# A two-layer attention kernel on one core: the first layer's output goes to channel rows by DMA instead of by TensorE transposes

## What is computed

```python
# layer 0
xm  = rmsnorm(x) * (1 + scale) + shift          # scale, shift from cond @ w_cond
q, k, v = split(xm @ w_qkv); q, k = rope(q), rope(k)
o   = softmax(q k^T / 4) v                      # per batch and head, 512 x 512 scores
x1  = o @ w_out + x
# layer 1
q, k, v = layer_norm(x1) @ (q_w, k_w, v_w) + biases
y   = softmax(q k^T + mask) v
out = x1 + silu(layer_norm(y) * (1 + scale1) + shift1) @ out_w + out_b
```

## Time and profile before

| | |
|---|---|
| median of 3 runs | 514.0 us (513.84 to 514.3) |
| the profiled execution | 513.65 us |
| its span, first to last instruction | 511.9 us |
| PE, PE's weight loads, DVE, ACT, POOL busy | 501.6, 193.7, 408.6, 345.7, 219.9 us |
| mean granted TensorE clock | 0.997 |

### The profile page before, as it was taken

The page is one execution under the profiler, slowest core; times in us unless marked ns, Lnnn a source line. Parts: engine busy times, 40 slices in busy tenths (PEclk is TensorE's granted clock), DMA queues, the critical chain, the costliest instruction groups (busy, mean ns, idle before and its releaser), DMA issues.

```text
span 511.9 us, 9839 instructions
## 1 busy us (share of the span) xinstructions
PE 501.6 (98%) x3339; PEld 193.7 (38%) x3339; DVE 408.6 (80%) x1051; ACT 345.7 (68%) x679; POOL 219.9 (43%) x254
## 2 busy tenths in 40 slices
PE   9999899999999999999999999999999999999997
PEld 5553423333443244333443334332433333333234
DVE  4876897998897688966898678967899999999324
ACT  1552467776767675776768676777778778787863
POOL 3039749999143420832227430544573035005401
PEclk9999999999999999999999999999999999999999
DMA  6983232242214133110331123210431112211011
GB/s 243 351 273 101 75 103 75 66 143 82 77 53 125 41 125 121 46 43 8 119 125 44 42 90 114 68 33 32 125 124 44 43 43 85 81 46 44 2 41 42
DMA packets 43034, 45.26 MB, mean 88 GB/s; under 512 B 4436, under 2 KB 41572, under 8 KB 42600
## 3 DMA queue, kind: packets, MB, share of 16 engines
q1 hardware_dynamic: 42696, 42.79, 26.8%
q10 hardware_dynamic: 288, 1.84, 0.9%
HBM read 25.46 MB, written 18.87 MB: 87 GB/s over the span
## 4 chain that ended last, share of the span: by engine, by line
PE 74%; DVE 13%; issue 3%; ACT 2%; POOL 2%; DVEq 0%; ACTq 0%; POOLq 0%
PE bank L547 19%; PE bank L530 11%; PE bank L521 10%; PE bank L593 9%; PE bank L510 9%; DVE masked L870 8%; PE bank L621 5%; PE bank L604 5%; PE bank L562 2%; PE bank L582 2%; DVE row_max L873 1%; ACT probs L721 1%; PE bank L555 1%; PE bank L629 1%; POOL XN L844 1%
## 5 line engine op out<-in xcount | busy, mean ns | idle before, releaser
L721 ACT ACTIVATE probs<-bank 128x512 f32<-128x512 f32 x512 | 272.4, 601 | 82.0 <-PE bank L521 81.3
L873 DVE TENSOR_REDUCE row_max<-bank 128x1 f32<-128x512 f32 x256 | 163.0, 684 | 29.5 <-PE bank L530 27.8
L530 PE MATMUL bank<-k_s,q_s 64*128 64x512 f16 x512 | 183.0, 382 | 1.8 <-DVE row_max L873 1.2
L870 DVE CUSTOM_DVE_ANT_0 masked<-bank,mask_bias 128x512 bf16<-128x512 f32 x256 | 163.0, 687 | 13.0 <-PE bank L530 12.0
L510 PE MATMUL bank<-q_s,k_s 64*128 64x512 f16 x512 | 151.9, 381 | 0.9 <-ACT v_aug L789 0.5
L521 PE MATMUL bank<-shift,kx 64*128 64x512 f16 x512 | 148.8, 377 | 0.0
L547 PE MATMUL bank<-probs,v_aug 128*17 128x512 f32 x1024 | 135.4, 598 | 0.7 <-ACT probs L721 0.7
L530 PEld LDWEIGHTS bank<-k_s,q_s 64*128 64x128 f16 x512 | 46.3, 93 | 151.7 <-DVE row_max L870 67.1
L593 PE MATMUL bank<-xT,wqkv 128*128 128x512 f32 x128 | 61.8, 613 | 0.4 <-ACT xT L752 0.3
L521 PEld LDWEIGHTS bank<-shift,kx 64*128 64x128 f16 x512 | 46.9, 95 | 31.9
L510 PEld LDWEIGHTS bank<-q_s,k_s 64*128 64x128 f16 x512 | 31.7, 94 | 13.4 <-ACT probs L721 8.0
(11 more groups left out here) (112 smaller groups left out, 505.1 us busy)
## 6 DMA issues: line engine op xcount, KB each, us to landing
q_parts<-parts SPq DMA_DIRECT2D x64, 128.0 KB
k_parts<-parts SPq DMA_DIRECT2D x64, 128.0 KB
q_s<-q_parts SPq DMA_DIRECT2D x32, 256.0 KB, 2.8
k_s<-k_parts SPq DMA_DIRECT2D x32, 256.0 KB, 3.0
X<-in_x SPq DMA_DIRECT2D x4, 512.0 KB, 7.3
y<-X SPq DMA_DIRECT2D x7, 256.0 KB, 2.2
wc<-in_w_cond ACTq DMA_DIRECT2D x1, 1024.0 KB, 4.9
tables<-in_tables SPq DMA_DIRECT2D x4, 256.0 KB, 6.8
```

The source lines that it names most:

```text
L530: nc.tensor.matmul(bank, m.q_s[slot][rows, i, queries], m.k_s[slot][rows, i, :], start=True, stop=True).then_inc(q.d_made, 1)
L721: act.activation(m.probs[k][:, h, :], bank, ACT.Exp, scale=1.0 if s >= B * NG else float(DH) ** -0.5)\
L870: dve.tensor_tensor_reduce(m.masked[D["max", n, k, h] % ND][:, :], bank, m.mask_bias[:, b, :], 1.0, LOWEST, ALU.add, ALU.max, to)\
L873: dve.tensor_reduce(to, bank, AX.X, ALU.max).then_inc(q.d_done, 1)
```

## The change

1. **No turns for layer 0's output.** Of groups 0 to 15 the output is no longer transposed. SP sends `oT` as it stands, 4 transfers of 16 rows by 2 KB, to rows of the tile `raw` (the old `O` buffers in another shape), where each channel has its own row, and one small transfer that lays out the 64 rows' sums as 128x16 (`raw_output`). DVE takes their reciprocal at tile k = 3 (`invert`). SP stores the reciprocals to DRAM (`inverses_out`) and loads them spread over the channels' rows (`inverses_in`). POOL multiplies, two products of 128x512 a batch (`divide`), straight into `xT`. The eight transposes of `turn f0` and their ACT copies are gone too.
2. **Where the products stand.** `y` of batch b moves from (5+4b, 2) and (5+4b, 3) to (6+4b, 0) and (6+4b, 1), and waits for `divided`, not for ACT. `turn p1`, `qk` and `v` of layer 1 move about three tiles later.
3. **POOL sends the parts.** The stores of `parts` of the batches 1 to 7, 4 for each of 28 calls, are issued by POOL behind each rope and split. Those of batch 0 stay with SP.
4. **Two `divide` in the rope list** (behind the second and third rope of batch 3), two in each `project(b)` below the last, and `add_bias(LAST, 1)` goes behind the first `negate`.

```diff
+    PIECES[_s] = (*one(y(0, _b)), _other, ())
+    PIECES[_s + 1] = ((), (), turn("p1", _b), qk(1, _b, 0))
+    PIECES[_s + 2] = (*one(qk(1, _b, 1, 2)), qk(1, _b, 3), ())
+    PIECES[_s + 3] = (v(1, _b)[:1], (), (), ())
+PIECES[20] = (*one(qk(1, LAST, 1, 2)), qk(1, LAST, 3), v(1, LAST)[:1])
+PIECES[21] = (v(1, LAST)[1:], (), (), ())
...
-        if op == "output" and k == 2 and s:
+        if op == "output" and k == 2 and s > LAYER:
             yield op, s - 1
+        if op == "output" and k == 3 and 0 < s <= LAYER:
+            yield "sums", s - 1
...
     def tokens_out(piece):
-                pe.wait_ge(q.a_done, turned(USES[use]))
+                pe.wait_ge(q.divided, normalised(b, CT - 1))
...
+    def invert(s):
+        dve.wait_ge(q.sums_in, 16 * (s + 1))
+        if s:
+            dve.wait_ge(q.inv_out, 16 * s)
+        dve.reciprocal(m.inv_sum[:, :, :, :].rearrange("p t h w -> p (t h w)"), m.sums[:, :]).then_inc(q.inv_made, 1)
...
+    def send_parts(pu, i):
+        send_part(pool, m, q, pu, i, 0)
+        pool.wait_ge(q.part_pool, 4 * (pu - 1) + i + 1)
+        send_part(pool, m, q, pu, i, 1)
...
+    def divide(b, c):
+        use = USES.index(("f0", b))
+        pool.wait_ge(q.output_out, group_out(NG * b + 2 * c + 1))
+        pool.wait_ge(q.inv_in[c], 32 * (b + 1))
+        await_read(pool, q, use - 2)
+        pool.tensor_tensor(m.xT[use % 2][:, c, :], m.raw[b % 2][:, c, :], m.inverse[c][:, :], ALU.mult)\
+            .then_inc(q.divided, 1)
...
             rope(b, i)
+            if b == B - 1 and i in (1, 2):
+                divide(0, i - 1)
...
+    def raw_output(s):
+        b, g = divmod(s, NG)
+        sp.wait_ge(q.acc_copied, s + 1)
...
+        sp.dma_start(m.sums[:, :], m.oT[DH::W32, :].rearrange("h (c n) -> h c n", n=KT * G)).then_inc(q.sums_in, 16)
...
+            sp.dma_start(m.raw[b % 2][first + DH * h:first + DH * (h + 1), g // 2, :],
+                         m.oT[W32 * h:W32 * h + DH, :]).then_inc(q.output_out, 16)
...
     for s in range(-1, GROUPS + 2):
+        if 0 < s <= LAYER:
+            raw_output(s - 1)
         if exists(s + 1):
             shift(s + 1)
         if s >= 0 and exists(s + 3):
             operands(s + 3)
-        for pu, i in PARTS_AT.get(s, ()):
-            parts(pu, i)
+        if 0 < s <= LAYER:
+            inverses_out(s - 1)
+        if 0 < s <= LAYER:
+            inverses_in(s - 1)
```

More of the change, by code:

```diff
@@ L29 @@
 GROUPS = LAYERS * B * NG
+LAYER = B * NG
 UNIT = 64.0
@@ L388, in build @@
         q.acc_copied = sem("acc_copied")
+        q.output_out = sem("output_out")
+        q.sums_in = sem("sums_in")
+        q.inv_out = sem("inv_out")
+        q.inv_in = [sem(f"inv_in{i}") for i in range(CT)]
+        q.divided = sem("divided")
         q.shift_high = sem("shift_high")
@@ L447, in build @@
         q.x_in = [sem(f"x_in{b}") for b in range(B)]
+        q.first_out = [sem(f"first_out{i}") for i in range(4)]
         q.parts_out = [sem(f"parts_out{i}") for i in range(4)]
@@ L480, in d_bank, with await_parts @@
     return m.d_banks[place % ND]
-def chunk_out(pu):
-    return 64 * (pu + 1)
+def await_parts(engine, q, pu, i):
+    if pu:
+        engine.wait_ge(q.parts_out[i], 64 * pu)
+    else:
+        engine.wait_ge(q.first_out[i], 64)
 def half(h):
@@ L567, in turn_tokens @@
         bank = d_free(D[piece]) if kind == "f1" else a_free(A[piece])
-        if kind == "f0":
-            pe.wait_ge(q.d_done, D["output", NG * b + NG - 1] + 1)
-            src = m.O[b % 2]
-        else:
-            n = NORMAL.index((kind, b))
-            src = m.XN[n % 2]
-            if h == 0 and n == 0:
-                pe.wait_ge(q.ident_made, 4)
-                pe.wait_ge(q.xn0_made, TPB)
-            elif h == 0 and n == len(NORMAL) - 1:
-                pe.wait_ge(q.xn0_made, 2 * TPB)
-            elif h == 0:
-                pe.wait_ge(q.xn_made, TPB * n)
+        n = NORMAL.index((kind, b))
+        src = m.XN[n % 2]
+        if h == 0 and n == 0:
+            pe.wait_ge(q.ident_made, 4)
+            pe.wait_ge(q.xn0_made, TPB)
+        elif h == 0 and n == len(NORMAL) - 1:
+            pe.wait_ge(q.xn0_made, 2 * TPB)
+        elif h == 0:
+            pe.wait_ge(q.xn_made, TPB * n)
         for t in range(TPB):
@@ L1074, in vector @@
                 negate(n)
+        if op == "sums":
+            invert(*at)
         if op == "output":
@@ L1244, in project @@
         normal("p1", b)
+        if b < LAST:
+            divide(b + 1, 0)
         at = m.X[:, TPB * b:TPB * b + TPB, :]
@@ L1253, in project @@
         add_bias(b, 0)
+        if b < LAST:
+            divide(b + 1, 1)
     pool.wait_ge(q.late_in, 64)
@@ L1258, in gpsimd @@
         project(b)
-    add_bias(LAST, 1)
     def negate(n):
@@ L1276, in gpsimd @@
         negate(NG * (B + b) + 6)
+        if b == 0:
+            add_bias(LAST, 1)
         rstd("f1", b)
@@ L1292, in gpsimd @@
             .then_inc(q.last_rstd, 1)
-def send_parts(engine, m, q, pu, i):
-    for part in range(2):
-        send_part(engine, m, q, pu, i, part)
 def send_part(engine, m, q, pu, i, part):
@@ L1306, in send_part @@
         to = m.k_dram[pu, heads, copy, part, dims, :] if i >= 2 else m.q_dram[pu, heads, part, copy, dims, :]
-        engine.dma_start(to, m.parts[:, part, i, :]).then_inc(q.parts_out[i], 16)
+        engine.dma_start(to, m.parts[:, part, i, :]).then_inc((q.parts_out if pu else q.first_out)[i], 16)
 def sync(sp, m, q):
@@ L1359, in shift, with inverses_out, inverses_in @@
                 .then_inc(q.shift_in[n % SHIFTS], 16)
+    def raw_output(s):
+        b, g = divmod(s, NG)
+        sp.wait_ge(q.acc_copied, s + 1)
+        if b >= 2:
+            sp.wait_ge(q.divided, normalised(b - 2, g // 2))
+        if s:
+            sp.wait_ge(q.inv_made, s)
+        sp.dma_start(m.sums[:, :], m.oT[DH::W32, :].rearrange("h (c n) -> h c n", n=KT * G)).then_inc(q.sums_in, 16)
+        first = chunk_rows(g).start
+        for h in range(G):
+            sp.dma_start(m.raw[b % 2][first + DH * h:first + DH * (h + 1), g // 2, :],
+                         m.oT[W32 * h:W32 * h + DH, :]).then_inc(q.output_out, 16)
+    def inverses_out(s):
+        sp.wait_ge(q.inv_made, s + 1)
+        sp.dma_start(m.inv_dram[s].rearrange("h (c n) -> (h c) n", n=KT * G),
+                     m.inv_sum[:, :, :, :].rearrange("p t h w -> p (t h w)")).then_inc(q.inv_out, 16)
+    def inverses_in(s):
+        b, g = divmod(s, NG)
+        sp.wait_ge(q.inv_out, 16 * (s + 1))
+        sp.wait_ge(q.part_dve, 4)
+        if g % 2 == 0 and b:
+            sp.wait_ge(q.divided, normalised(b - 1, g // 2))
+        sp.dma_start(m.inverse[g // 2][chunk_rows(g), :], m.inv_dram[s].unsqueeze(1).broadcast_to([G, DH, S]))\
+            .then_inc(q.inv_in[g // 2], 16)
     def output(b, j):
```

56 lines of the change are left out of this document (29 added, 27 removed).

## The result

The changed kernel takes 516.15 us (median of 8 runs, 514.94 to 520.68) against 514.02 for the kernel before in the same session: a ratio of 1.0057, 95% interval 1.003 to 1.0085. It is slower, as forecast, but by 2.1 us and not by 9, and not for the reason that I gave. The profiled execution has a span of 514.3 us; before it was 511.9. One single run behind this page, of the second padding in experiment 2, took 623.17 us at a granted clock of 0.748, and its ratio leaves that run out.

The account below looks back on a forecast made before the run. PE was taken to bound the kernel, with 74% of the chain of waits. 513.65 - 12.1 (turns) + 18.3 (wait for `divide`) + 1.6 (group 22) + 1.5 (clock) = 523.0 us, range 502 to 534.

Parts of the forecast that it names:

- Twelve microseconds go from PE: PE, layer 0: 16 output turns at 0.5 us and four turns back, together 12.1 us gained.
- I take no more than 0.5 us off for that: DVE loses one 0.43 us product a group; where it bounds a plain step it gives back nearly the same.
- DVE above 13% of the chain, gain below 10: Sign in the profile after: if seen, with the gain being PE's, DVE's room was put too high.
- The new way if POOL were free: Output path through SP, DVE and reciprocals: ready near 133, PE at the product at 137.6; cost nothing.
- SP is the late one: Rival: SP blocked ahead of `shift`, PE waiting 1 to 2 us in 8 to 16 steps; 510 to 534 us; chance 0.06.
- POOL's price: POOL's time c to issue one store, 112 issues: taken as 0.95 us, from bounds 0.6 to 1.13.
- 18.3 us of the sum: First product with w_out: PE waits 18.3 us for POOL's second `divide`, which ends at 155.9.
- the rival: POOL's issue is cheap, c 0.6 or less: wait 0 to 3 us; 501.5 to 511 us; chance 0.30; decides at c = 0.78.
- POOL's half of that working: POOL's second `divide` at the first product with w_out ends at 114.1 + 44c, 155.9 with c = 0.95.
- PE's half, 137.6: PE reaches the first product with w_out at 137.6, against 135.45 in the kernel before.
- Group 22's negation, 1.6 us: Layer 1, batch 3: POOL's `negate` ends at 29.7, PE needs it at 28.1; one wait of 1.6 us.
- The clock, 1.5 us: Behind the 18 us wait PE's clock may start low, near 1.2 GHz, for two to four microseconds; cost 1.5 us.

Follow-up runs that it names:

- second padding: Kernel before, with SP issuing five extra transfers of 16 rows by 2 KB ahead of `shift` in steps 1 to 16: 518.1 us, ratio 1.0071.
- experiment 2: Kernel before, five extra SP transfers ahead of `shift` in steps 1 to 16: small ones 514.27 us, ratio 1.0002; 16 rows by 2 KB 518.1 us, 1.0071.
- exp. 3: Kernel before, one transpose in place of four in each output turn of groups 0 to 15 and each turn back: 510.62 us, ratio 0.9933.
- exp. 1: Changed kernel, SP's order with `raw_output` last: 518.86 us, ratio 1.0094; with `operands` first, then `shift`, `raw_output` (the version meant): 509.09 us, 0.9900.
- exp. 5: Kernel before with POOL sending parts, plus one wait on POOL: 515.4 us, ratio 1.0024. Changed kernel with two POOL fills behind each of twelve ropes: 529.51 us, 1.0296.
- exp. 6: Changed kernel, `operands` first, three POOL waits: 510.86 us, ratio 0.9936; with a fourth wait and second `divide` ahead of the third rope: 505.06 us, 0.9823.
- exp. 4: Kernel before with POOL sending the parts of batches 1 to 7: 517.24 us, ratio 1.006. Changed kernel with SP sending them again: 527.32 us, 1.0254.

## Why the prediction went wrong

**Twelve microseconds go from PE.** The instructions went. Their worth did not follow: "I take no more than 0.5 us off for that". PE's time alone reached the end at 3.6 of 9.1 us, or of 7.9 by the timelines (exp. 3); even the best version gets 9.0 of 12.1. The earlier trace rows had shown DVE busy 10.85 of 11.50 us, and I wrote down the limit, 0.65 us a step, and compared it with one turn of 0.5. It should have been read as: DVE already paces this step, through a loop in which each waits for the other in turn. The sign of it was on my own list (DVE above 13% of the chain, gain below 10), and it came: 17%.

**The new way if POOL were free: "I cost the change at nothing".** This is the step whose mechanism failed, by 7.1 us (exp. 1); the term that was off by most is POOL's price, below. I counted SP's issues, 3 us, and looked at one transfer behind them, `shift`, which has three tiles. The load behind `shift` was in SP's list, name both, and I called its need far: "a load every step stays far from its need". It is issued for group s + 3 in step s and read from tile (s + 1, 0) on, the next thing that PE does; its slack was 0.3 us (exp. 2). I also had no row for the traffic of POOL's stores beside it, with which its landing went from 3.07 to 4.27 us. "SP is the late one" stood among the rivals at 0.06, with the wrong queue member and a price of 8 to 32 us from 501.5. Its mechanism, PE waiting 1 to 2 us behind SP, is what the changed kernel does (waits of 0.17, 0.58, 2.11 and 1.14 us in four steps of the opening, of 1.86 and 0.69 in two later ones).

**POOL's price.** c was 0.95; it is 0.53 in a row of four and 0.58 by the mean. Of my two bounds the lower was right, and slightly too high. The choice of the upper half rested on POOL being 1.86 times slower than DVE at a product, and the issue is not such work. This one term carried 18.3 us of the sum, and measured 0: with c = 0.53 there is no wait for `divide`, as the rival said (decides at 0.78). The rival's time, 501.5 to 511, did not come either, since it took the rest of the working as it stood. That POOL's half of that working holds is shown by exp. 5 (156.0 against 155.9), and by exp. 6, where 3 us on POOL brought the wait; PE's half, 137.6, was reached only with both orders mended (138.04). The 0.607 us that the prediction set beside a time to the first byte is how long SP's queue is busy with an issue, and no row there shows a first byte; c is the busy time too.

**Group 22's negation, 1.6 us.** Not there: in the changed kernel PE waits nowhere for POOL's negation. It hung on the same c.

**The clock, 1.5 us.** Right in kind and near in size (1.7 us, an estimate from the two stretches at 0.61 and 0.54), but behind the load of the keys and not behind `divide`.

**What I did not have at all** is the collision of POOL's longer work with DVE's two small operations, 3.0 us for the sends alone (exp. 4), of which 1.8 were given back by one wait (exp. 5). The kernel before has it in small: one such operation took 0.86 us at 115.97.

**Sum.** The forecast had one large loss (18.3) against one large gain (12.1). In truth the gain that was to be had with this order on POOL was 4.9 us (exp. 1), the sends' collisions already inside it, and SP's order took 7.1; the difference is the measured +2.1, by the way the two are taken. The forecast's loss did not exist, a loss that it had at nothing stood in its place, and its gain was too large: that the direction came out right was luck. The range of 502 to 534 held the time; the chance of 0.60 for the forecast's own mechanism was far too high for a price that no row showed.

**What stays open.** The 3.1 us between 9.0 and 12.1 I put down to DVE's pace by exp. 3; no run relieved DVE further to show it. The runs of the changed kernel spread over 5.7 us, those of the version of experiment 1 over 0.2; the mean granted clock was 0.996 in the fastest of them and 0.986 in the slowest, against 0.993 in all four of the latter, so the clock has a part in it; what makes it fall in one run and not in another, no run shows.

## What to carry to other kernels

When transfers are put into a queue, look at every transfer behind them up to the next idle time, find for each the instruction that reads it, and compare its slack with the delay; the one directly behind is not the one that is late. Freed time of an engine is worth its length only in steps where no other engine's busy share is near one; try it by leaving the work out (3.6 of 9.1 us here). And before work is given to POOL, look for small SBUF operations of DVE on the critical path beside it: one wait that lets them through first gained 1.8 us; four and a moved product gained 4.0.

## What the hardware showed that I had not expected

- **POOL is no dearer than SP at issuing a store.** 0.53 us in a row of four (2.12 us), 573 and 585 ns by the mean, against 607 on SP for the same transfer; landing 2.9 to 3.0 us.
- **DVE's small operations can wait for POOL's, now and then also while POOL issues transfers.** 0.17 us became 0.95 beside issues and 1.21 beside a product, ending within 0.1 us of POOL's end both times. Thirteen that started 0.12 to 0.81 us into a row of issues in the changed kernel were not lengthened. Row maxima from PSUM stayed at 0.68 to 0.69 us.
- **PE's clock after a wait does not go by the wait's length alone.** After waits of 1.45, 1.66, 2.11, 3.36 and 9.84 us of PE the granted clock fell to 0.50 to 0.61 in a stretch of 2 us behind (0.50 behind the longest), and behind the two longest eight matmuls of 128x256 took 3.51 and 3.75 us instead of 1.99. But the changed kernel has a wait of 1.86 us for the keys that ends at 204.42, and the clock stays full behind it:

```profile
204.00:206.00 2.00, 1.58 (x7) 1.23 (x8) 0.69 (x1) 0.00 (x0) 0.00 (x0) 1.00 0.03 3
206.00:208.00 2.00, 2.00 (x18) 0.65 (x16) 1.23 (x3) 0.69 (x2) 0.00 (x0) 1.00 0.16 62
```

In the version with `raw_output` last a wait of only 0.76 us at 92.6 was followed by 0.50 from 94 to 96 us. I draw no rule from these rows.
- **A load's landing grew with its neighbours.** The load of the keys took 4.27 us beside 0.52 MB of POOL's stores, against 3.0 by the median of the kernel before, and 2.94 behind five transfers of the shape of `raw_output`'s without POOL's stores.
